# The edge stage of a graph layer: TensorE derives tile numbers in registers, ScalarE's copies take one loaded number a step

## The chip, the cores and the metric

The kernel runs on one core of a Trainium2 chip. The metric is the device time of one execution in microseconds (us). TensorE, VectorE, ScalarE and GpSimd are called PE, DVE, ACT and POOL, as in the profile; SP is the queue that only issues DMAs.
## The reference, cut to what matters

A layer over 6250 nodes with 512 features and 100000 edges sorted by their destination. It adds a graph attention term (the part at hand) and a linear attention term, and then a mixture of experts.

```
e      = leaky_relu(el[src] + er[dst])            # 8 heads
a      = exp(e - segment_max(e, dst)[dst])
denom  = segment_sum(a, dst);  msg = feat_v[src] * a / denom[dst]
x      = x + segment_sum(msg, dst) + linear_attention(layernorm(x))
x      = x + experts(layernorm(x))
```

## The kernel before, in words

Nodes are padded to 49 tiles of 128 rows (NT). Edges are cut into steps of 128 edges, so that no step crosses from one node tile into the next: 832 steps (ST), taken in 52 chunks of 16 (NCH, U). Tile numbers rise with the steps; a step that is the last of its tile is a "turn", and there are 48 turns inside the stage.

The program has a set-up, a projection of all 49 tiles (`proj`), a mix stage (`mix`), the **edge stage**, a join stage with routing, the experts and the output. The change is in the edge stage and in the tables that the set-up makes for it. Work in the edge stage is ordered by hand: every engine runs its own `chunk` function, a loop over two chunks a pass with the first and last two peeled (`chunks`, L114), and the engines meet at semaphores.

- POOL (`values`, L611 on, the DMA at L618) gathers 128 rows of `v_table` a step, 16 gathers a chunk into one half of `vg`. The gather for a step of chunk c waits for the same step of chunk c-2 on PE.
- DVE (`step`, L1186 on): every four steps it makes four one-hot matrices `hot` (L1189), and for each step it multiplies the gathered rows by their weights (L1182) and signals `step_pv`. Between the steps it runs the chain of small operations that makes the next chunk's weights: `scored` (after step 2), `run_max` (4), `linked` (6), `joined_max` (9), `shifted` (12), `factored` (14), `turned_hot` (15). `rescaled` (after step 1) takes the accumulator that PE closed with `acc_shut`, and scales it.
- PE (`step`, L1560 on): two f32 matmuls of 128x260 in four passes (L1566) add the step to the accumulator in one of two rooms of PSUM (tile number even or odd). It then branches on "turn" (L1569): a turn closes the room (`empty`, L1551) and opens the other. Between the steps PE does its part of the chain: `turned_e` (after step 1), `gathered_ends` (3), `spread_ends` (5), `turned_max` (8), `factors` (10). At a chunk's end it closes the accumulator for `rescaled`, and runs `expanded` for chunk c+2: 16 small matmuls, whose operand is addressed by the tile number of each step. At the next chunk's start it brings the scaled accumulator back in (L1581).
- ACT (`snapshots`, L748 on): for each step it copies an accumulator from PSUM to `fin` (L757). At a turn that is the finished tile; at any other step it copies a dummy bank, so that the program is the same for each. Before it the copy waits for four semaphores (L754 to L757). Between the copies ACT issues the loads of chunk c+2's locals and computes `factor` (after step 4, L741) and `weights` (after step 10, L745), which DVE needs for the next chunk's first step.
- SP (`tile_store`, L487) stores each finished tile from one of four slots of `fin`.

Numbers that depend on the data (where a step's accumulator lies, whether it is a turn, its tile) stand in tables in SBUF, one entry or more a step, and each engine loads them into registers with `looked_up` (L422, the load instruction has line L424):

```
marks[:] = looked_up(ENGINE.PE, pe_tab, t * 2, 2 * V + 1, 2 * D)        # PE: 9 numbers, 4 times a chunk
return looked_up(ENGINE.PE, d_tab, c * U, U, NT - 1)                     # PE: 16 numbers, once a chunk
places = looked_up(ENGINE.Activation, act_tab, t * 2, 2 * n, DUMMY * D)  # ACT: 2n numbers for n steps
counts = looked_up(ENGINE.Activation, act_tab, t * 2 + 2 * ST, 2 * n, 32768)
```

PE and DVE also load the chunks' base from `chunk_tab` (three numbers every two chunks), and PE loads one number at a turn. DVE makes the tables in the set-up (L943 to L984), 1x832 operations one behind the other.

## Time and profile before

| | us |
|---|---|
| median of 3 runs (lowest to highest) | 3522.52 (3513.96 to 3525.18) |
| the profiled execution, its own time | 3480.26 |
| its span, first to last instruction | 3478.4 |
| busy PE / DVE / POOL / ACT | 2417.5 / 1829.6 / 1338.1 / 909.8 |
| mean granted share of PE's clock | 0.809 |

The span is the time between the first and the last instruction of the profiled execution. Busy is the time in which an engine ran instructions; work of the sequencers is not counted in it. "Idle before" is the time in which an engine had nothing to run ahead of an instruction, with what ended it; "issue" there means that nothing which the profile shows was waited for, so that the engine's own sequencer was late. A granted clock of 1.00 is PE at full clock.

### The profile page before, as it was taken

Reading aid. Unit: us, or ns where it says so; the run is one execution under the profiler, and the core shown is the slowest. Engines: PE = TensorE matmul, PEld = TensorE weight load, DVE = VectorE, ACT = ScalarE, POOL = GpSimd, SP = SyncE. Lnnn points to the kernel's source line nnn. Section 1 sums busy time; section 2 is a strip of 40 time slices with the busy share of each in tenths; the row PEclk is TensorE's granted clock in tenths of the full one; section 3 lists DMA queues with packets and bytes.
Section 4 is the critical chain, followed back from the end, with each engine's and each line's share of the span. In section 5 each row is a group of like instructions: output and inputs, shape, how many; then the busy total and the mean of one; then the engine's idle time right before and its main releaser. Section 6 shows DMA issues by size and latency. Waiting matters only on the chain. (4 is left out here: it accounts for less than half of the span.)

```text
span 3478.4 us, 50828 instructions
## 1 busy us (share of the span) xinstructions
PE 2417.5 (69%) x11245; PEld 1803.3 (52%) x11246; DVE 1829.6 (53%) x3903; ACT 909.8 (26%) x1917; POOL 1338.1 (38%) x1406
## 2 busy tenths in 40 slices
PE   3899998666777877777877777777233329999500
PEld 3677776223555555555555555555233328888400
DVE  5544443786666655566556655565353334444433
ACT  0111111011333333333333333333443313333100
POOL 0000000302565555565556555652144342222244
PEclk8899998898888878888788878889555559999755
DMA  3122222644555555655656556653655634444576
GB/s 115 49 68 68 68 68 77 228 167 134 165 162 159 157 164 163 169 160 154 169 164 171 166 154 173 170 163 89 221 134 136 131 76 134 145 145 145 168 257 232
DMA packets 238264, 507.89 MB, mean 146 GB/s; under 512 B 50320, under 2 KB 76432, under 8 KB 238208
## 3 DMA queue, kind: packets, MB, share of 16 engines
q0 software_dynamic: 85936, 274.85, 28.6%
q1 hardware_dynamic: 134752, 196.94, 18.5%
q10 hardware_dynamic: 17520, 35.44, 3.0%
q8 instruction: 24, 0.39, 0.1%
q14 instruction: 32, 0.26, 0.0%
HBM read 394.73 MB, written 112.37 MB: 146 GB/s over the span
## 5 line engine op out<-in xcount | busy, mean ns | idle before, releaser
L618 POOL DMA_INDIRECT arena<-v_table,idx x832 | 917.2, 1102 | 847.1 <-PE ps L1566 670.1
L1566 PE MATMUL ps<-arena 128*128 128x260 f32 x3328 | 975.4, 441 | 315.9 <-issue 289.6
L1566 PEld LDWEIGHTS ps<-arena 128*128 128x128 f32 x3328 | 678.5, 216 | 533.2 <-issue 427.7
L757 ACT ACTIVATE arena<-ps x832 | 501.9, 603 | 1096.2 <-PE ps L1566 668.4
L1182 DVE TENSOR_TENSOR arena<-arena 128x512 f32<-128x512 f32 x832 | 547.1, 683 | 0.0
L1384 PE MATMUL ps<-arena 128*128 (+4 forms) x1994 | 423.8, 336 | 94.3 <-DMA arena<-q_table 73.8
L1389 PE MATMUL ps<-ident,arena 128*128 128x128 f32 x1128 | 213.8, 308 | 328.1 <-DVE arena L1257 257.2
L1384 PEld LDWEIGHTS ps<-arena 128*128 128x128 f32 (+1 forms) x1994 | 275.7, 195 | 224.8 <-issue 115.3
L1389 PEld LDWEIGHTS ps<-ident,arena 128*128 128x128 f32 x1128 | 151.0, 159 | 349.3 <-DVE arena L1257 262.2
L658 POOL DMA_INDIRECT arena<-xn_table,e_idx x105 | 99.3, 945 | 281.5 <-PE ps L1389 265.0
L595 POOL TENSOR_SCALAR ag<-ag 128x1 f32<-128x1 f32 x49 | 10.7, 219 | 502.3 <-DVE ag L999 502.2
L1189 DVE TENSOR_TENSOR arena<-col_no,arena 128x512 f32<-128x512 f32 x208 | 142.2, 684 | 106.2 <-ACT arena L745 55.2
L1336 DVE TENSOR_TENSOR xt_lo<-ps,xt_hi 128x512 fp32r<-128x512 f32 x105 | 72.6, 692 | 213.3 <-ACT xt_hi L824 213.3
L1182 DVE TENSOR_TENSOR arena<-ps,r_all 128x512 f32<-128x512 f32 x51 | 35.3, 692 | 219.2 <-PE ps L1551 219.2
L669 POOL DMA_INDIRECT arena<-y_table,slot_of x98 | 100.3, 1024 | 127.4 <-DVE arena L1375 74.8
L801 ACT ACTIVATE arena<-arena,r_den 128x64 f32<-128x64 f32 x392 | 98.6, 334 | 162.4 <-DVE r_den L1242 162.2
L1384 PE MATMUL ps<-w_hi,xt_hi 128*128 x420 | 129.1, 307 | 2.6 <-DVE xt_lo L1336 2.6
L1581 PE MATMUL ps<-arena,ident 128*128 128x260 f32 x204 | 103.3, 661 | 37.0 <-issue 32.3
L1239 DVE TENSOR_SCALAR r_den<-arena 128x8 f32<-128x8 f32 x49 | 8.4, 171 | 228.0 <-DMA arena<-agg 227.8
L1384 PE MATMUL ps<-w_hi,xt_lo 128*128 x420 | 119.5, 284 | 0.0
L1384 PE MATMUL ps<-w_lo,xt_hi 128*128 x420 | 118.2, 281 | 0.0
L635 POOL DMA_INDIRECT token_of<-token_no,slot_of x98 | 102.0, 1041 | 25.6 <-issue 25.6
(282 smaller groups left out, 3470.0 us busy)
## 6 DMA issues: line engine op xcount, KB each, us to landing
y_table<-arena SPq DMA_DIRECT2D x105, 256.0 KB, 2.5
arena<-local_table ACTq DMA_DIRECT2D x52, 512.0 KB, 4.2
arena<-in_x SPq DMA_DIRECT2D x98, 256.0 KB, 2.7
arena<-v_table,idx POOLq DMA_INDIRECT x832
v_table<-arena SPq DMA_DIRECT2D x49, 260.0 KB, 2.9
agg<-arena SPq DMA_DIRECT2D x49, 260.0 KB
arena<-agg SPq DMA_DIRECT2D x49, 260.0 KB, 4.6
x_mix<-arena SPq DMA_DIRECT2D x49, 256.0 KB, 2.7
```

The source lines that it names most:

```text
L618: pool.indirect_dma_start(vg[:, j % 2 * U + i, :], None, v_table, bass.IndirectOffsetOnAxis(ap=idx[:, j, i:i + 1], axis=0))\
L635: pool.indirect_dma_start(token_of, bass.IndirectOffsetOnAxis(ap=slot_of[:, t, k:k + 1], axis=0), token_no[:, t:t + 1], None).then_inc(s(" ...
L658: pool.indirect_dma_start(xg[:, j % 4, :], None, xn_table, bass.IndirectOffsetOnAxis(ap=e_idx[:, j:j + 1], axis=0)).then_inc(s(f"eg_in{j % ...
L669: pool.indirect_dma_start(cy[:, j * TOP + k, :], None, y_table, bass.IndirectOffsetOnAxis(ap=slot_of[:, t, k:k + 1], axis=0)).then_inc(s(f ...
L757: act.activation(halves(fin[:, bass.ds(dst_, DH)], HALF), halves(ps[:, bass.ds(src_, 2 * D)], D)[:, :, 0:HALF], ACT.Copy).then_inc(s("act_ ...
L801: last = act.activation(da[:, j, cols], da[:, j, cols], ACT.Copy, scale=r_den[:, j, h:h + 1])
L1182: return dve.tensor_tensor(out_[:, :, 0:D // 2].rearrange("p i (h f) -> p i h f", h=H // 2), in_[:, :, 0:D // 2].rearrange("p i (h f) -> p ...
L1189: dve.tensor_tensor(hot[:, i // V % 2], col_no[:].unsqueeze(1).broadcast_to([P, V, P]), dst_local[:, bass.ds(t, V)].unsqueeze(2).broadcast ...
L1384: last = pe.matmul(dst, a, b, start=(opened and i == 0), stop=(closed and i == n - 1))
L1389: last = pe.transpose(dst[:, c * P:(c + 1) * P], src[:, c * P:(c + 1) * P], ident[:])
L1566: last = pe.matmul(ps[:, bass.ds(acc + h * D, HALF)], hot[:, i // V % 2, i % V, :], vg[:, b * U + i, h * HALF:(h + 1) * HALF], start=False ...
L1581: pe.matmul(ps[:, bass.ds(base + h * D, HALF)], ident[:], acc_kept[:, h, :], start=True, stop=False)
```

## The change

Tables: `pe_tab`, `act_tab`, `d_tab` and `chunk_tab` go; `first_tab` (the tile of each chunk's first step), `turn_tab` (16 turn bits of each chunk) and `room_tab` (one number a step: the room at a turn, the dummy bank otherwise) come. `tile_tab` gets an entry ahead and an offset. PE works out each step's turn, tile and room from the chunk's first tile and its bits. ACT loads 16 numbers once a chunk; the number is the address of both source and target, so `fin` has two slots in place of four. The copy of step t waits for PE's step t+1, and no longer for `tile_sum` and `fin_st`; PE waits for `fin_st` at a turn instead. The chain operations stand at other steps. DVE's first `hot` of a chunk is ahead of the wait for the weights.

```diff
-def chunks(eng, body, bases=None):
+def chunks(eng, body, places, ahead):
     for c in range(2):
-        body(c, c, 0, *(bases(c, 2) if bases else ()))
+        body(c, c, 0, places(c, ahead + 1))
     with eng.Fori(1, NCH // 2 - 1) as i:
-        own = bases(i * 2, 3) if bases else ()
+        own = places(i * 2, ahead + 2)
         for j in range(2):
-            body(i * 2 + j, j, i, *own[j:j + 2])
+            body(i * 2 + j, j, i, own[j:j + ahead + 1])
...
+def turn_of(eng, bits, i):
+    return eng.snap((bits >> i) & 1, min_val=0, max_val=1)
+def room_of(eng, d):
+    return eng.snap((d & 1) * (2 * D), min_val=0, max_val=2 * D)
+def next_tile(eng, d, turn):
+    return eng.snap((d + turn).with_bounds(min_val=0, max_val=NT - 1))
...
+        def chunk_places(engine, c, n):
+            return list(zip(looked_up(engine, first_tab, c, n, NT - 1), looked_up(engine, turn_tab, c, n, 2 ** U - 1)))
...
-                sp.dma_start(rows(agg, d), fin[:, j * DH:(j + 1) * DH]).then_inc(s("fin_st"), 16)
+                sp.dma_start(rows(agg, d), fin[:, j * 2 * D:j * 2 * D + DH]).then_inc(s("fin_st"), 16)
...
-            def snapshots(t, n):
-                places = looked_up(ENGINE.Activation, act_tab, t * 2, 2 * n, DUMMY * D)
-                counts = looked_up(ENGINE.Activation, act_tab, t * 2 + 2 * ST, 2 * n, 32768)
-                for i in range(n):
-                    (src_, dst_), (closed, stored) = places[2 * i:2 * i + 2], counts[2 * i:2 * i + 2]
-                    act.wait_ge(s("step_mm"), t + (i + 1))
-                    if later(t, 1) or i:
-                        act.wait_ge(s("act_step"), t + i)
-                    act.wait_ge(s("tile_sum"), closed)
-                    act.wait_ge(s("fin_st"), stored)
-                    act.activation(halves(fin[:, bass.ds(dst_, DH)], HALF), halves(ps[:, bass.ds(src_, 2 * D)], D)[:, :, 0:HALF],
-                                   ACT.Copy).then_inc(s("act_step"), 1)
+            def snapshot(t, room):
+                if later(t, 1):
+                    act.wait_ge(*past("act_step", t))
+                act.wait_ge(s("step_mm"), t + 2)
+                act.activation(halves(fin[:, bass.ds(room, DH)], HALF), halves(ps[:, bass.ds(room, 2 * D)], D)[:, :, 0:HALF],
+                               ACT.Copy).then_inc(s("act_step"), 1)
...
+                rooms = looked_up(ENGINE.Activation, room_tab, c * U, U, DUMMY * D)
+                for i in range(U):
+                    snapshot(c * U + i, rooms[i])
+                    if not more:
+                        continue
+                    if i == 8:
+                        factor(c + 1)
+                    elif i == 11:
+                        weights(c + 1, 1 - b)
...
                 for i in range(U):
-                    step(c * U + i, i, b)
+                    if i % V == 0:
+                        found(c * U + i, i)
+                    if i == 0:
+                        dve.wait_ge(s("p_exp"), c + 1)
+                    step(i, b)
                     if i == 1 and later(c, 1):
-                        rescaled(c, base)
+                        rescaled(c, room_of(dve, own[0][0]))
...
-                    if i == 2:
+                    if i == 5:
                         scored(c + 1, n, q)
-                    elif i == 4:
+                    elif i == 7:
                         run_max(c + 1, n)
-                    elif i == 6:
+                    elif i == 9:
                         linked(c + 1)
-                    elif i == 9:
+                    elif i == 11:
                         joined_max(c + 1, n)
-                    elif i == 12:
+                    elif i == 13:
                         shifted(c + 1, n)
...
-                for i, d in enumerate(tiles):
+                for i in range(U):
                     last = product(prep[:, i * 3 * H:(i + 1) * 3 * H],
-                                   [(hot_t[:, i * P:(i + 1) * P], er_flat[:, bass.ds(d * 3 * H, 3 * H)])])
+                                   [(hot_t[:, i * P:(i + 1) * P], er_flat[:, bass.ds(d * (3 * H), 3 * H)])])
+                    if i < U - 1:
+                        d = next_tile(pe, d, turn_of(pe, bits, i))
...
-            def step(t, i, b):
-                if i % V == 0:
-                    marks[:] = looked_up(ENGINE.PE, pe_tab, t * 2, 2 * V + 1, 2 * D)
-                acc, turn, other = marks[i % V * 2:i % V * 2 + 3]
+            def step(t, i, b, d, turn):
+                acc = room_of(pe, d)
                 pe.wait_ge(s("step_pv"), t + 1)
...
+                other = ((acc + 2 * D) & (4 * D - 1)).with_bounds(min_val=0, max_val=2 * D)
                 with pe.If(turn):
-                    empty(acc, False, True).then_inc(s("tile_sum"), 1)
-                    freed, = looked_up(ENGINE.PE, pe_tab, t + (2 * ST + 2), 1, ST)
+                    empty(acc, False, True)
+                    pe.wait_ge(s("fin_st"), d * 16 + past("fin_st", -16)[1])
+                    freed, = looked_up(ENGINE.PE, tile_tab, d, 1, past("act_step", ST)[1])
                     pe.wait_ge(s("act_step"), freed)
                     empty(other, True, False)
...
-                    if i == U - 1 and ahead:
-                        tiles = tiles_of(c + 2)
-                    step(c * U + i, i, b)
+                    turn = turn_of(pe, bits, i)
+                    step(c * U + i, i, b, d, turn)
+                    d = next_tile(pe, d, turn)
                     if not more:
                         continue
-                    if i == 1:
+                    if i == 5:
                         turned_e(c + 1)
-                    elif i == 3:
+                    elif i == 7:
                         gathered_ends(c + 1)
-                    elif i == 5:
+                    elif i == 9:
                         spread_ends(c + 1)
-                    elif i == 8:
+                    elif i == 11:
+                        factors(c + 1)
+                    elif i == 12:
                         turned_max(c + 1)
-                    elif i == 10:
-                        factors(c + 1)
```

In the set-up, 23 operations over all 832 steps (L947 to L981) become 9, with a reduction to 52 numbers, 16 one-element memsets and a few small copies beside them.

## Rows read from the trace of the kernel before

**Rows 1.** The page: the span, and PE's granted clock in 40 slices, in tenths

```profile
span 3478.4 us, 50828 instructions
PEclk8899998898888878888788878889555559999755
```

**Rows 2.** Waits in the edge stage, 900 to 2370 us: total, times, longest

```profile
ACT arena L757 <- PE ps L1566: 598.4, 330, 6.9
POOL arena L618 <- PE ps L1566: 462.2, 288, 8.0
PE ps L1566 <- issue: 274.9, 186, 3.9
DVE arena L1182 <- PE ps L1551: 207.9, 47, 6.1
DVE arena L1130 <- DMA arena<-v_table,idx: 144.9, 47, 5.4
DVE arena L1189 <- ACT arena L745: 46.8, 24, 2.4
```

**Rows 3.** Line L424, one chunk, 1133 to 1163.5 us

```profile
L424 ACTq TENSOR_LOAD <-arena x11: 468/1717/1751, 1134.1 to 1163.4; - x11
L424 PEldq TENSOR_LOAD <-arena x7: 288/2157/3792, 1133.1 to 1157.6; - x7
```

**Rows 4.** Timeline of PE: start us, us, what, idle before in brackets

```profile
1120.33 1.92 PE L1566 MATMUL ps<-arena 128*128 128x260 f32 x8
1129.38 1.14 PE L1566 MATMUL ps<-arena 128*128 128x260 f32 x4 [2.93 <-issue]
```

**Rows 5.** Lines L1564 (in a PE step) and L1384 (in expanded), short windows

```profile
L1564 PEldq ALU_OP  x3: 36/36/36, 1155.5 to 1156.8; - x3
L1384 PEldq FUSED_REGOPS  x16: 64/64/74, 1130.3 to 1132.5; - x16
```

**Rows 6.** Line L1566: matmuls of 1138 to 1142 and of 1150 to 1153 us

```profile
L1566 PE MATMUL ps<-arena x8: 640/641/802, 1137.4 to 1141.9; 128*128 128x260 f32 x8
...
L1566 PE MATMUL ps<-arena x11: 382/383/482, 1149.7 to 1152.8; 128*128 128x260 f32 x11
```

**Rows 7.** Stretches of one chunk: busy of PE, PEld, DVE, ACT, POOL, PEclk, DMA

```profile
1124.00:1134.00 10.00, 5.87 (x34) 3.94 (x32) 3.84 (x8) 4.03 (x8) 6.94 (x8) 0.89 0.73 195
1134.00:1146.00 12.00, 10.92 (x27) 6.85 (x27) 4.87 (x12) 2.08 (x4) 2.86 (x3) 0.52 0.41 130
1146.00:1154.00 8.00, 7.42 (x33) 5.63 (x33) 7.37 (x20) 3.10 (x7) 5.99 (x5) 1.00 0.55 141
```

**Rows 8.** Groups of instructions in the edge stage, 900 to 2370 us

```profile
L1566 PE MATMUL ps<-arena 128*128 128x260 f32 x3020 | 893.0, 444 | 294.2 <-issue 274.9 <-DVE arena L1182 19.2
L618 POOL DMA_INDIRECT arena<-v_table,idx x753 | 834.7, 1108 | 621.0 <-PE ps L1566 462.2 <-issue 158.8
L757 ACT ACTIVATE arena<-ps x753 | 454.2, 603 | 1002.6 <-PE ps L1566 598.4 <-issue 214.4 <-ACT arena L757 82.8
L1182 DVE TENSOR_TENSOR arena<-arena 128x512 f32<-128x512 f32 x755 | 497.1, 683 | 0.0
L1159 DVE TENSOR_TENSOR_SCAN arena<-arena,f_l 128x128 f32<-128x128 f32 x47 | 22.8, 484 | 5.1
```

**Rows 9.** Line L745, one instruction a chunk, 52 in all

```profile
L745 ACT ACTIVATE arena<-arena x52: 301/301/310, 826.3 to 2407.1; 128x128 f32<-128x128 f32 x52
```

**Rows 10.** Timeline of DVE in the set-up: first and last operation on the tables

```profile
73.89 0.58 DVE L947 TENSOR_SCALAR arena<-arena 1x832 f32<-1x832 f32 x1
92.51 0.19 DVE L983 CAST arena<-ps 1x48 uint16<-1x48 f32 x1
```

**Rows 11.** Timeline at the end of the edge stage

```profile
2431.16 0.39 PE L1551 MATMUL ps<-zeros 1*128 1x260 bf16 x2
2438.36 0.60 ACT L757 ACTIVATE arena<-ps  x1 [0.66 <-ACT arena L757]
2441.02 5.67 SPq L500 DMA_DIRECT2D arena<-in_w  x4
```

More of the change, by code:

```diff
@@ L779, in _ @@
             weights(0, 0)
-            chunks(act, chunk)
+            chunks(act, chunk, lambda c, n: (None,) * n, 0)
             act.wait_ge(s("step_mm"), ST)
@@ L981, in _ @@
-            step_of(dve.tensor_copy(pe2[:, :, 1], turn))
+            step_of(dve.tensor_scalar(odd, odd, float(2 * D), -float(DUMMY * D), ALU.mult, ALU.add))
+            step_of(dve.tensor_tensor(odd, odd, turn, ALU.mult))
+            step_of(dve.tensor_scalar(room_tab[0:1, :], odd, float(DUMMY * D), None, ALU.add))
+            step_of(dve.memset(turn[:, ST - 1:ST], 0.0))
+            power_row, bits = odd[:, 0:U], odd[:, U:U + NCH]
+            for i in range(U):
+                last = dve.memset(power_row[:, i:i + 1], float(2 ** i))
@@ new lines, in _ @@
+            step_of(last)
+            in_chunks = [row_.rearrange("o (c i) -> o c i", i=U) for row_ in (turn, aux)]
+            step_of(dve.tensor_tensor(in_chunks[1], in_chunks[0], power_row.unsqueeze(1).broadcast_to([1, NCH, U]), ALU.mult))
+            step_of(dve.tensor_reduce(bits, in_chunks[1], AX.X, ALU.add))
+            dve.tensor_copy(turn_tab[0:1, 0:NCH], bits)
+            dve.memset(turn_tab[0:1, NCH:NCH + 2], 0)
+            dve.tensor_copy(first_tab[0:1, 0:NCH], d_r[:, 0:ST:U])
@@ L1226, in _ @@
             turned_hot(1, 1, 0)
-            chunks(dve, chunk, lambda c, n: looked_up(ENGINE.DVE, chunk_tab, c, n, 2 * D))
+            chunks(dve, chunk, lambda c, n: chunk_places(ENGINE.DVE, c, n), 0)
             def weights_lo(c):
@@ L1604, in _ @@
             pe.wait_ge(s("er_split"), 5)
[L1605 removed]
+            begun = chunk_places(ENGINE.PE, 0, 2)
+            expanded(0, *begun[0])
             turned_e(0)
@@ L1609, in _ @@
             turned_max(0)
-            expanded(1, tiles_of(1))
-            empty(0, True, False).then_inc(s("tile_sum"), 1)
-            chunks(pe, chunk, lambda c, n: looked_up(ENGINE.PE, chunk_tab, c, n, 2 * D))
-            empty((NT - 1) % 2 * 2 * D, False, True).then_inc(s("tile_sum"), 1)
+            expanded(1, *begun[1])
+            empty(0, True, False)
+            chunks(pe, chunk, lambda c, n: chunk_places(ENGINE.PE, c, n), 2)
+            pe.wait_ge(*past("fin_st", 16 * (NT - 2)))
+            empty((NT - 1) % 2 * 2 * D, False, True).then_inc(s("step_mm"), 1)
             def logits(t):
```

125 lines of the change are left out of this document (45 added, 80 removed).

## The prediction

> **What bounds the kernel now.** First the page: span 3478.4 us, with PE's granted clock at 0.8 to 0.9 of full through the edge stage [rows 1]. The execution's own time, 3480.3 us, is 42 us under the median of the runs, 3522.5; I make the sum against 3480.3 and move it by the difference. The line of `weights` comes once a chunk and gives the stage its measure: 1580.8 us for 51 intervals, **31.0 us a chunk** [rows 9].
>
> Then the waits, to see who is late [rows 2]. ACT and POOL wait for PE. DVE waits for PE too: 207.9 us, 4.4 a chunk, until PE has closed the accumulator. It also waits 3.1 a chunk for the gather, and 1.0 for ACT's exponential. PE waits for "issue", 274.9 us or 5.8 a chunk. Nothing else in the profile is late there: PE's own sequencer is. What it does shows on the load line, in one chunk [rows 3]. Four loads of nine numbers take 2.16 us each, one of 16 takes 3.79, one of a single number 0.29. That is about 0.23 us a number beyond the first, so the three-number load is near 0.75. Together 8.63 + 3.79 + 0.29 + 0.75 = 13.5 us of a 30.5 us chunk go to loading numbers. Some of it hides behind queued matmuls, but where matmuls are short or few, PE runs dry: 2.93 us before step 15, during the load of 16 [rows 4].
>
> ACT is second. It makes twelve loads a chunk: six of eight numbers at 1.72, four of two at 0.47 [rows 3], two of four at 0.88 between them; 14.0 us. With 16 copies at 0.60 [rows 8] that is 23.7 us before any wait, and so it is often behind.
>
> Last, the clock [rows 7]. Around the chunk's end PE has little work; after it, 12 us run at 0.52, near 1.2 GHz, and then 8 us at 1.00. A matmul takes 641 ns there and 383 ns else [rows 6]. The mean of 444 [rows 8] puts 24% of them, 15 of 64 a chunk, in the slow stretch. Back to back at full clock they come every (1.92 - 0.38)/7 = 0.22 us [rows 4], so 15 slow ones cost 3.3 us a chunk.
>
> **The change part by part.**
>
> *PE's loads.* Gone: 13.5 us a chunk, but for the one number at a turn. New: eight numbers every two chunks, as two loads of four, each 0.29 + 3 x 0.23 = 0.98, so 1.0 us a chunk. Net -12.2 us of sequencer.
>
> *PE's register work.* A step gains two operations for the turn bit, two for the room and one for the next tile; each of the 16 matmuls of `expanded` gains three. The trace has no bit operation, so I bound it. Below: register work that rides in one instruction with other register work is cheap, since the address instructions of `expanded` take only 64 to 74 ns where a single operation takes 36 [rows 5]; at some 12 ns an operation that is 0.06 us a step, 0.04 a small matmul. Above: each one alone. A single one takes 36 ns and a gap to the next instruction; the step's own four instructions recur every 0.65 us, a branch of 0.2 among them, so about 0.10 each, 0.5 a step and 0.3 a matmul; with two more for the other room, if they are made at each step, 0.7. I take 0.16 and 0.08, nearer the lower end, because rows 5 show compound register instructions wherever this kernel computes an address. Sum 16 x 0.24 = 3.8 us a chunk; bounds 1.6 and 16.
>
> PE's sequencer then: 30.5 less the waits, which I put at 3.8 in this chunk (what is left when steps at 0.65, loads and the rest are laid end to end), gives 26.7; minus 12.2, plus 3.8: **18.3 us**. It is no longer the limit.
>
> *What is late next.* PE's array: 64 matmuls at 0.22 are 14.1 us. Bringing the accumulator back is 0.9. `expanded` is 2.3 [rows 5] + 1.3. The five small products, the closings and the turn are about 4, an estimate from their 0.2 to 0.4 us a piece. That is **22.6 us** at full clock. On top come hand-overs. The chain operations used to stand three or four steps apart between PE and DVE (`turned_e` after step 1, `run_max` after 4; 8 and 12 for the maximum). They now stand two apart and finally one (12 and 13). So PE waits where DVE is inside `joined_max`: two scans of 0.48 and small ones, near 2 us, then one-hots and a product at 0.68 each [rows 8], while PE has one small product; 2.5 us. Likewise 1.2 us around `run_max`. Sum 3.7. Of the slow clock's 3.3 us I keep half, 1.7, because the thin stretch ahead of it shortens by the load of 16 and of three but does not go. New chunk: 22.6 + 3.7 + 1.7 = **28.0 us**, against 31.0.
>
> *ACT.* Loads 14.0 to one of 16 numbers: 0.47 + 14 x 0.21 = 3.4. Also 11 fewer address instructions and two fewer waits a step. It costs nothing as long as ACT stays behind PE: 3.4 + 9.7 + waits is far below 28. The load sits after the chunk's two DMA issues, so ACT starts each chunk some 5 us late; `factor` after copy 8 hides that. If the cover fails, `joined_max` waits for `factor`, which needs PE's step 9: 1 us at most, inside the 2.5 above. Copying a step later adds one step before a room is free; the shortest tiles are about 8 steps, so nobody waits. PE's new wait for `fin_st` asks for a tile stored two turns ago; queued behind it are the opening of the room and the next step, but the wait is met. Both 0.
>
> *DVE.* One-hots ahead of the wait for the exponential take up its 1.0 us. `scored` after step 5 instead of 2 gives the gather three more steps, about 2.6 us, against 3.1 us of wait. Both gains fall to DVE, which is not the bound; they are inside the 28.0 and I add nothing.
>
> *POOL and SP.* No instruction more. POOL is released by PE's steps and follows them. Its floor is 16 x (1.108 + 0.34 between two, 158.8/465) = 23.2 us a chunk [rows 2, 8], under 28.0. SP's stores are as many and as large.
>
> *Set-up.* The tables take 73.89 to 92.70, 18.8 us of DVE alone, with the first projection behind them [rows 10]. New: nine at 0.6 to 1.05 us, a reduction, 16 memsets and copies, 10.2 by those prices. **-8.6 us**; if the memsets cost 0.2 each, -6.
>
> *End of the stage.* PE's last instruction ends at 2431.6, ACT's last copy at 2439.0, and SP's weight loads start at 2441.0 [rows 11]. With ACT one copy behind PE, that shrinks from 7.4 to about 1: **-6.4 us**. Behind it is the last tile's store, as before.
>
> Sum: 51 x 3.0 = 153, + 8.6 + 6.4 = **168 us**; 3480.3 - 168 = 3312, and by the same 168 from the median, **3354 us**.
>
> **The rivals.**
>
> *A. PE stays at full clock and the chunk falls to POOL's pace.* The thin stretch is shorter, and if that is enough for PE never to fall to 1.2 GHz, the slow clock's rest goes too, and with loosely coupled hand-overs the chunk meets POOL's 23.2 to 25 us. For: 5.8 us a chunk of issue waits go. Against: `expanded` with its few columns stays, and 2 us of waiting are added in the middle. Time: 31.0 - 24.5 = 6.5 x 51 = 332 + 15: 3175 us.
> The Trainium skill ("TensorE: Matmul & The Clock Gate", Part 1) says the array's slow clock is the default and that only activity lifts it. By that rule a denser PE gains beyond the time saved; the rows 7 agree that thin work precedes the slow stretch, and whether it is thin enough here no row of the kernel before can say.
>
> *B. The hand-overs eat it.* The closer chain costs 6 us and the slow clock stays whole: 22.6 + 5.5 + 3.3 is 31.4, no gain in the stage. For: DVE already waits for PE at 4.4 us a chunk. Time: the ends alone, 3507 us, and up to 3525.
>
> *C. Slower: register work takes the loads' place.* Mechanism: bit operations don't join others, so that a step's sequence is 0.65 + 0.7 us, above the array's 0.88. PE's sequencer is then 26.7 - 12.2 + 16 = 30.5 us a chunk with nothing prefetchable, and about 2 us of the hand-overs lie bare: 32.5, +1.5 x 51 - 15 = +61: 3584 us. It decides from about 0.6 us of added register time a step. For: no row shows a bit operation. Against: rows 5.
>
> That the change doesn't do what it says is no case of weight: the loads go, by the code.
>
> **How the numbers follow.** Forecast 0.51 (27 to 30 us a chunk: 3305 to 3455), A 0.21, B 0.14, C 0.14. A measurement here tells about 0.3%, 10.5 us, from no change. Faster: forecast, A, and about half of B (3507 is 0.4% down) = 0.79; same 0.07; slower 0.14. The range of eight in ten reaches from **3200**, which leaves out the lower part of A, to **3520**, the middle of B; the forecast alone is 3305 to 3455.
>
> **What would show it.** Right: loads of PE and ACT down to under 1.5 and 3.5 us a chunk; `weights` every 28 us; PE's "issue" waits mostly gone; new waits of PE for DVE's `joined_max` and of DVE for PE's transposes; tables at 10 us; ACT's last copy 1 to 2 us after PE. If step-to-step on PE's sequencer is over 1.1 us, C is at work. If the chunk is under 26 us and the clock near 1.00, A. If the chunk is 31 with loads gone, B, and the wait that holds it is on the list of waits by name. The prediction is wrong in kind if ACT, slowed by its one load, holds a room that PE needs.

## The result, and the profile after

The changed kernel is **slower**: 3643.24 us in the median of four runs (3637.65 to 3653.28) beside 3518.80 (3513.96 to 3525.18) for the kernel before, a ratio of 1.036 with a 95% interval of 1.032 to 1.039. (The 3522.52 from which the prediction starts is the median of three of the same four runs.) The forecast was 3354 in a range of 3200 to 3520.

One warning on the sets of runs. Each set ran on one chip, with the kernel before beside it. In this set and in the fifth below the kernel before took 3512 to 3519 us, in the four between (on three chips) 3478 to 3485. The changed kernel stood at 1.036 here and, measured twice more, at 1.014 and 1.013 on chips of the other kind. The profiled execution of before took 3480.3 us, so its trace is comparable with the traces of the four sets between. Below, the sign and the mechanism are read from those, and the first trace of the changed kernel is given beside them.

The page of the changed kernel's first trace, its span, clock, and the groups that answer to [rows 8]; the last line is the scan that begins DVE's part of the chain:

```profile
span 3635.5 us, 53428 instructions
...
PEclk8999997997888887887878888878755558999855
...
L637 POOL DMA_INDIRECT arena<-v_table,idx x832 | 860.6, 1034 | 1070.5 <-PE ps L1563 837.3
L1563 PE MATMUL ps<-arena 128*128 128x260 f32 x3328 | 990.5, 451 | 180.2 <-DVE arena L1180 98.3
...
L770 ACT ACTIVATE arena<-ps x832 | 502.7, 604 | 1250.9 <-PE ps L1563 945.5
...
L1180 DVE TENSOR_TENSOR arena<-arena 128x512 f32<-128x512 f32 x832 | 539.0, 684 | 0.0
...
L1133 DVE TENSOR_TENSOR_SCAN arena<-arena,ps 128x128 f32<-128x128 f32 x52 | 21.9, 421 | 406.1 <-issue 259.1
```

The work is the same. DVE's and ACT's operations take as long as before; the matmul's mean is 451 ns, after 441 on the page of before (444 in the window of [rows 8]), and the gather's 1034 after 1102 there. POOL and ACT mainly wait longer. The line of `weights`, in the first trace of the changed kernel and then in its third measurement, on a chip where before takes 3478:

```profile
L764 ACT ACTIVATE arena<-arena x52: 301/302/310, 827.3 to 2577.3; 128x128 f32<-128x128 f32 x52
```

```profile
L764 ACT ACTIVATE arena<-arena x52: 301/302/310, 818.6 to 2470.2; 128x128 f32<-128x128 f32 x52
```

That is (2577.3 - 827.3)/51 = **34.3 us a chunk** and (2470.2 - 818.6)/51 = **32.4**, against 31.0 [rows 9] and the 28.0 of the forecast. The loss is there. In the third measurement, on a chip like that of before's trace, the span grew by 45.9 us (3524.3 for 3478.4): the 51 intervals give 70.8, the first `weights` comes 7.7 earlier, and what follows the last one is 17.2 shorter. The first trace's span grew by 157 us with 51 x 3.3 = 168 in the intervals, but it is from the chip on which before itself takes 38 us more, so that sum holds the chip's part too.

What took the place of the old waits? The waits of the edge stage, 900 to 2300 us, in the third measurement (us in total, times, longest):

```profile
ACT arena L770 <- PE ps L1563: 900.1, 343, 11.8
POOL arena L637 <- PE ps L1563: 523.6, 271, 10.8
DVE arena L1133 <- PE ps L1533: 340.6, 43, 11.8
...
PE ps L1563 <- DVE arena L1180: 152.4, 95, 2.7
...
DVE carry L1150 <- ACT factor_h L760: 70.1, 43, 3.4
DVE arena L1162 <- PE ps L1545: 69.4, 43, 3.3
...
PE ps L1582 <- issue: 58.9, 29, 2.8
PE ps L1386 <- issue: 47.0, 284, 0.3
...
DVE arena L1180 <- PE ps L1552: 30.8, 28, 3.0
...
PE ps L1563 <- issue: 0.5, 3, 0.2
```

PE's "issue" waits in the steps are gone, 0.5 us where [rows 2] have 274.9, and DVE hardly waits for the closed accumulator (30.8 for 207.9). At the end of a chunk PE still waits for its own sequencer: 1.4 us a chunk before the scaled accumulator is brought back (58.9 us; 30.0 before, 0.6 a chunk) and 1.1 in `expanded` (47.0). In place of the old waits stands a chain of hand-overs: DVE waits 7.9 us a chunk (340.6/43.2) for PE's turned scores, 1.6 for ACT's factor, 1.6 for PE's turned maximum, and PE 3.5 for DVE's products. In the kernel before, DVE's wait for the factor was next to nothing, 0.07 us a chunk. The same row of its waits, 900 to 2370 us:

```profile
DVE carry L1152 <- ACT factor_h L741: 3.5, 5, 1.1
```

The sequencer of PE in the changed kernel: the branch at the end of a step, in steps that follow one another, and the register work of `expanded` (a chunk's 16 small matmuls):

```profile
L1567 PEldq COMPARE_BRANCH  x8: 207/207/207, 1688.4 to 1695.5; - x8
...
L1386 PEldq ALU_OP  x29: 3/36/341, 1613.8 to 1618.9; - x29
L1386 PE MATMUL ps<-arena x16: 173/184/200, 1614.0 to 1619.1; 128*128 x16
```

Steps recur every (1695.5 - 1688.4)/7 = 1.01 us, small matmuls every (1619.1 - 1614.0)/15 = 0.34, where [rows 5] give 2.2/15 = 0.15.

The loads, over 900 to 2400 us, PE's and ACT's:

```profile
L439 PEldq TENSOR_LOAD <-arena x80: 3/981/997, 965.8 to 2389.1; - x80
...
L439 ACTq TENSOR_LOAD <-arena x44: 3374/3400/4355, 905.7 to 2387.6; - x44
```

Set-up and end of the stage, to [rows 10, 11]: the first and the last operation on the tables, then PE's last instruction and SP's weight loads.

```profile
73.65 0.58 DVE L957 TENSOR_SCALAR arena<-arena 1x832 f32<-1x832 f32 x1
...
82.57 0.20 DVE L981 TENSOR_SCALAR arena<-ps 1x48 uint16<-1x48 f32 x1
...
2598.34 0.39 PE L1552 MATMUL ps<-zeros 1*128 1x260 bf16 x2
...
2602.09 2.08 SPq L519 DMA_DIRECT2D arena<-in_w  x3
```

The tables take 9.1 us for 18.8, the stage's end 3.8 for 9.9. Both are close to the prediction (9.7 us gained for 8.6, 6.1 for 6.4), and the 16 memsets are one row of 0.21. But on the first chip the first `weights` starts at 827.3 for 826.3: nothing of the 9.7 us reached the edge stage there, while in the third measurement it starts at 818.6.

### The profile page after: what moved, and what is told of

Same layout as the page of the kernel before. It is cut to its first block, busy times and chain, and to the rows that moved or that the text cites. A ratio compares the mean times of both kernels' runs of the same rounds, so it can differ in the third digit from the quotient of the medians.

```text
span 3635.5 us, 53428 instructions
## 1 busy us (share of the span) xinstructions
PE 2503.5 (69%) x11245; PEld 1857.2 (51%) x11246; DVE 1828.1 (50%) x3907; ACT 911.4 (25%) x1917; POOL 1288.9 (35%) x1406
## 3 DMA queue, kind: packets, MB, share of 16 engines
q1 hardware_dynamic: 134752, 196.94, 17.7%
## 4 chain that ended last, share of the span: by engine, by line
PE 23%; DMA 9%; issue 8%; DVE 8%; POOL 1%; SPq 1%; another core or an unknown queue 1%; ACT 1%; ACTq 1%; DVEq 0%; POOLq 0%
PE ps L1386 11%; PE ps L1563 9%; DMA arena<-agg 5%; DMA arena<-y_table,slot_of 3%; PE ps L1391 2%; DVE arena L1180 1%; DVE bn L1252 1%; PE ps L1582 1%; POOL arena L688 1%; DVE arena L1250 1%; PE ps L1552 1%; DVE arena L1259 1%; DVE arena L1374 1%; DVE arena L1377 1%
## 5 line engine op out<-in xcount | busy, mean ns | idle before, releaser
L637 POOL DMA_INDIRECT arena<-v_table,idx x832 | 860.6, 1034 | 1070.5 <-PE ps L1563 837.3
L1563 PE MATMUL ps<-arena 128*128 128x260 f32 x3328 | 990.5, 451 | 180.2 <-DVE arena L1180 98.3
L1563 PEld LDWEIGHTS ps<-arena 128*128 128x128 f32 x3328 | 711.3, 225 | 380.5 <-issue 258.0
L1386 PE MATMUL ps<-arena 128*128 (+4 forms) x1994 | 495.6, 336 | 228.8 <-issue 96.7
L1180 DVE TENSOR_TENSOR arena<-arena 128x512 f32<-128x512 f32 x832 | 539.0, 684 | 0.0
L1386 PEld LDWEIGHTS ps<-arena 128*128 128x128 f32 (+1 forms) x1994 | 296.4, 192 | 404.1 <-issue 313.6
L1133 DVE TENSOR_TENSOR_SCAN arena<-arena,ps 128x128 f32<-128x128 f32 x52 | 21.9, 421 | 406.1 <-issue 259.1
```

The source lines that it names most:

```text
L637: pool.indirect_dma_start(vg[:, j % 2 * U + i, :], None, v_table, bass.IndirectOffsetOnAxis(ap=idx[:, j, i:i + 1], axis=0))\
L1180: return dve.tensor_tensor(out_[:, :, 0:D // 2].rearrange("p i (h f) -> p i h f", h=H // 2), in_[:, :, 0:D // 2].rearrange("p i (h f) -> p ...
L1386: last = pe.matmul(dst, a, b, start=(opened and i == 0), stop=(closed and i == n - 1))
L1563: last = pe.matmul(ps[:, bass.ds(acc + h * D, HALF)], hot[:, i // V % 2, i % V, :], vg[:, b * U + i, h * HALF:(h + 1) * HALF], start=False ...
```

## The experiments

Two theories to begin with. **The order**: the chain's places were moved, so that PE and DVE stand two steps apart and less, and the hand-overs lie bare. **The register work**: bit operations that stand alone take the place of the loads. Each run's chunk is the span of its `weights` line over 51, read from one trace. The edits are shown in short form.

### First set: which part of the change costs (before: 3484.65 us)

**e1_moved**, the kernel before with the five places of PE and of DVE and the two of ACT as the change has them, and PE's loads as before. ACT's numbers are the same 64 a chunk, but in ten loads for twelve, since its copies are grouped around other places:

```diff
 PE:   i == 1, 3, 5, 8 (maximum), 10 (factors)  ->  5, 7, 9, 12 (maximum), 11 (factors)
 DVE:  i == 2, 4, 6, 9, 12                      ->  5, 7, 9, 11, 13
 ACT:  factor after copy 4, weights after 10    ->  factor after copy 8, weights after 11
```

> The kernel before, with only the places of the chain operations moved as the change moves them (PE 5, 7, 9, 11, 12; DVE 5, 7, 9, 11, 13; ACT's factor after copy 8, its weights after copy 11); tables and loads as before. The changed kernel's chunk is 34.3 us against 31.0, +3.3, though its sequencer's loads went. Theory O (order): the closer hand-overs cost the time, so this kernel is slower than before as well, by 3 us a chunk or more: over 3670 us against 3519. Theory R (register work): the order is worth nothing or a gain, and the register instructions cost the time: 3519 within 1%, or below. If both have a share, it lies between, and the share is read off.

Measured: 3568.44 us, 1.024 (1.022 to 1.026), chunk 32.75. The order costs 1.75 us a chunk without any of the register work.

**e2_order_back**, the changed kernel at the old places:

```diff
-    PE 5, 7, 9, 11 (factors), 12 (maximum); DVE 5, 7, 9, 11, 13; ACT factor after copy 8, weights after 11
+    PE 1, 3, 5, 8 (maximum), 10 (factors); DVE 2, 4, 6, 9, 12; ACT factor after copy 4, weights after 10
```

> The changed kernel, with the chain operations back at their old places (PE 1, 3, 5, 8, 10; DVE 2, 4, 6, 9, 12; ACT 4 and 10). Theory O: the hand-overs loosen, and what is left is the gain of the loads: 28 to 30 us a chunk, 3360 to 3460 us. Theory R: a chunk stays near 34 us, 3640 us within 1%, because PE's step has a pitch of 1.02 us in its sequencer where it had 0.61, and a small matmul of the expansion 0.34 where it had 0.14, wherever the chain stands.

Measured: 3411.30 us, 0.979 (0.977 to 0.980), chunk 30.04. Its wait of PE for the joined maximum and of DVE for the factor, 900 to 2300 us:

```profile
PE ps L1545 <- DVE arena L1157: 111.9, 47, 4.2
...
DVE carry L1150 <- ACT factor_h L760: 71.1, 39, 3.1
```

The rest of the change is a gain once the places are the old ones. But DVE's wait for the factor is already here, 1.5 us a chunk, so it isn't only the order that makes it.

**e3_arith**, the changed kernel with the bit operations written as arithmetic:

```diff
-    (bits >> i) & 1          (d & 1) * (2 * D)   (acc + 2 * D) & (4 * D - 1)
+    bits // 2 ** i % 2       (d % 2) * (2 * D)   acc * -1 + 2 * D
```

> The changed kernel, with the shift and the bit operations written as divisions, remainders and products, which can share one register instruction. Theory R: the steps' pitch falls from 1.02 toward 0.8 us, the small matmuls' from 0.34 toward 0.25, some 5 us a chunk off the sequencer, and most of it shows: 3400 to 3500 us. Theory O: the chunk gains less than 1.5 us, since PE's sequencer waits in the hand-overs: above 3560 us.

Measured: 3537.06 us, 1.016 (1.014 to 1.017), chunk 32.29. The changed kernel itself had 32.40 and 1.014 in the next set. Cheaper register work brings next to nothing in the changed order.

**e4_pe_loads**, the changed kernel with PE's numbers loaded from tables again; `step` takes three numbers of nine, `expanded` 16 tile numbers. The eight numbers every two chunks of the changed kernel stay beside them (before loads three there), and a turn loads two numbers for one:

```diff
-                acc = room_of(pe, d)
+                if i % V == 0:
+                    marks[:] = looked_up(ENGINE.PE, pe_tab, t * 2, 2 * V + 1, 2 * D)
+                acc, turn, other = marks[i % V * 2:i % V * 2 + 3]
```

> The changed kernel, with PE's numbers loaded from tables again (nine numbers four times a chunk, sixteen once), and ACT's single load, two slots and the new order kept. Theory R: PE's register work is gone, ACT is relieved: at or below the kernel before, 3400 to 3520 us. Theory O: the new order alone makes it slow: above 3600 us, since the loads come back on top.

Measured: 3582.20 us, 1.029 (1.027 to 1.030), chunk 33.26: 0.86 over the changed kernel, 0.51 over e1_moved. Against e1_moved it has ACT's new part, and no gain of it shows. What the 0.51 belongs to isn't separated: PE's further loads come to some 0.9 us of its sequencer a chunk, an estimate from the 0.98 us of a load of four, the 0.75 of one of three and the 0.29 of one number.

### Second set: the lead, and what each part brings in the old order (before: 3482.11 us)

**e5_after**, the changed kernel itself, no edit.

> The changed kernel itself, beside the others on one chip, so that all stand against the same kernel before. 34.3 us a chunk, ratio 1.036 as before; no theory expects otherwise.

Measured: 3533.70 us, 1.014 (1.013 to 1.016), chunk 32.40. The loss is real on this chip too, but under half of what the first one showed.

**e6_loose**, PE's places earlier, DVE's left as changed:

```diff
-    PE 5, 7, 9, 11 (factors), 12 (maximum); factor after copy 8
+    PE 4, 6, 8, 9 (factors), 10 (maximum);  factor after copy 6
```

> The changed kernel, with DVE's chain as late as the change puts it (5, 7, 9, 11, 13), but PE's share earlier, at 4, 6, 8, 9 and 10 in place of 5, 7, 9, 11 and 12, and ACT's factor after copy 6 in place of 8. So DVE may again be three steps ahead of PE where it had two, and in the end one. Theory L (lead): the new order costs time because DVE may not run ahead of PE far enough: this gives most of the 4.3 us a chunk back, 30 to 31.5 us a chunk, ratio 0.98 to 1.00. Theory D (depth): it costs because the chain begins so late that it ends past the chunk, whatever the lead: 33 to 34.3 us a chunk, ratio above 1.02.

Measured: 3409.85 us, 0.979 (0.978 to 0.981), chunk 29.92: all that e2_order_back gives.

**e7_loads_back** is e4_pe_loads at the old places (diffs of e4_pe_loads and e2_order_back).

> PE's numbers loaded from tables, the old order, ACT's single load: so the kernel before with the new ACT part and set-up. If ACT's loads had a part in the 31.0 us, this is below before: 29 to 30.5 us a chunk, ratio 0.96 to 0.98, and then PE's registers bring nothing by themselves beside the 30.0 us of the changed kernel in old order. If PE's sequencer alone was the bound, it stays at 30.5 to 31.5, ratio 0.99 to 1.01, and the 1.0 us gained is the registers'.

Measured: 3504.35 us, 1.006 (1.005 to 1.008), chunk 31.63. It is the kernel before with the new set-up, DVE's one-hots and ACT's part, and with more loads on PE: 322 in 900 to 2300 us, 7.3 a chunk, where before has 288, 6.4 a chunk. Its chunk is 0.6 us longer than the 31.0 of before. So eleven loads less a chunk on ACT show no gain, though PE's extra loads may hide one. From here to e2_order_back (30.04) it is 1.6 us a chunk for PE's registers; from the kernel before, with its fewer loads, to e2_order_back it is 1.0.

**e8_arith_back** is e3_arith at the old places.

> The old order with division and remainder in place of shift and bit operations. In the new order that rewriting was worth 2.0 us a chunk. If PE's sequencer is still in the path in the old order, it gives 1 to 2 us again: 28 to 29 us a chunk, ratio 0.95 to 0.965. If the path now runs through the array, DVE and the hand-overs, under 0.5 us: ratio 0.97 to 0.98.

Measured: 3380.77 us, 0.971 (0.969 to 0.973), chunk 29.32. In the old order the cheaper register work is worth 0.7 us a chunk; in the changed one 0.1. The branch of its steps, one after the other:

```profile
L1567 PEldq COMPARE_BRANCH  x7: 203/207/207, 1601.7 to 1606.9; - x7
L1567 PEldq FUSED_REGOPS  x6: 107/107/107, 1601.5 to 1606.0; - x6
```

A step takes (1606.9 - 1601.7)/6 = 0.87 us of the sequencer for 1.01.

### Third set: which hand-over (before: 3478.92 us)

**e9_turn4** moves one place of PE, **e10_max10** two, **e11_arith_loose** joins e3_arith and e6_loose, and **e12_inif_back** is e8_arith_back with the other room computed inside the branch:

```diff
 e9:   -    i == 5: turned_e                  +    i == 4: turned_e
 e10:  -    i == 11: factors, 12: turned_max  +    i == 9: factors, 10: turned_max
 e12:  -    other = (acc * -1 + 2 * D) ...    (ahead of the branch)
       +        other = (acc * -1 + 2 * D) ...    (in it)
```

> The changed kernel with one place altered: PE turns the scores over after step 4, not 5; the other four places of PE stay. The profile of the changed kernel has DVE standing 338.3 us (7.2 a chunk) at the running maximum until that turn, and PE standing 153.6 us for DVE's products. Theory of the lead (the first hand-over carries it: what DVE loses there PE pays back later in the chunk): the turn comes one step earlier, about 1 us a chunk of DVE's stand goes, and the chunk falls from 32.4 to about 31.4, ratio to before about 1.00. Rival (the last hand-over carries it, the maximum turned after step 12 right behind the factors): the first place is worth nothing, the chunk stays at 32.4, ratio 1.014. Theory of the register work (PE's sequencer paces): no change either.

Measured: 3542.65 us, 1.019 (1.017 to 1.020), chunk 32.59. No gain. Its waits, 900 to 2300 us, say where it went:

```profile
DVE arena L1133 <- PE ps L1533: 286.1, 42, 10.6
...
DVE carry L1150 <- ACT factor_h L760: 118.2, 43, 4.1
```

DVE's largest wait fell from 7.9 to 6.7 us a chunk, and its wait for ACT's factor rose from 1.6 to 2.8. The wait of 7.9 us, which I had taken for the cost, can thus be cut by 1.2 without a gain, as long as the factor comes late. ACT comes next.

> The changed kernel with the end of the chain alone brought forward on PE: factors after step 9, behind the spread ends, and the turned maximum after step 10, not 11 and 12. Theory of the first hand-over: DVE makes the maximum at its step 11 only, after its long stand, so PE now waits for it at step 10 with nothing gained for DVE; chunk 32.4 or some tenths more, ratio 1.01 to 1.02. Rival (last hand-over): DVE's stand for the turned maximum (64.9 us, 1.4 a chunk) and PE's stand at the steps behind it (153.6 us, 3.3 a chunk) go, chunk about 30, ratio about 0.98.

Measured: 3483.03 us, 1.002 (1.001 to 1.003), chunk 31.46. The rival's direction, at two fifths of its size.

> Two edits of earlier runs together: the five places of PE brought forward (0.979 alone) and the bit operations written as division, remainder and product (1.0156 against 1.0143 in the changed order, so nothing there; 0.971 against 0.979 in the old order). If the register work counts only where the hand-overs leave PE the last to arrive, this order gives what the old one gave: about 0.971, chunk 29.2. If the places brought forward have made DVE the last to arrive, the register work is hidden and it stays at 0.979, chunk 29.9.

Measured: 3393.85 us, 0.976 (0.974 to 0.977), chunk 29.64: between the two.

> The fastest version so far (old order, arithmetic in place of bit operations, 0.971, chunk 29.3) with the two operations for the other room moved into the branch that needs them, so that only a turn makes them. It takes about 2 x 0.1 us from PE's sequencer at 14 or so of 16 steps, 2.9 us a chunk. Theory of the register work: PE's sequencer still sets part of the chunk, 0.5 to 1.5 us a chunk go, ratio 0.95 to 0.965. Rival (the array and the hand-overs set it): within 0.3% of 0.971.

Measured: 3374.10 us, 0.970 (0.969 to 0.972), chunk 29.32. Void as a test of register work: the order of instructions on PE is the same as in e8_arith_back, as far as the traces show: both have 50007 instructions, and ahead of each branch the same one of 107 ns. It stands as a second measurement of the fastest version.

### Fourth set: the place of ACT's factor (before: 3478.31 us)

```diff
 e13_factor6, on the changed kernel:
-                    if i == 8:
+                    if i == 6:
                         factor(c + 1)
```

**e14_factor6_max10** adds e10's edit to it; **e15_loose_factor8** is e6_loose with the factor left after copy 8; **e16_after** is the changed kernel.

> The changed kernel with ACT's factor after copy 6 instead of 8, nothing else. Copy 8 needs PE's step 9, and DVE's joined maximum behind its step 11 needs that factor: where PE's turn was moved to step 4, DVE's stand for the factor grew from 1.70 to 2.75 us a chunk and ate what was won. Theory of the closed ring (PE step 9, ACT's copy and factor, DVE's joined maximum and next product, PE step 12): the 1.7 us stand of DVE goes and with it 1 to 2 us of PE's 3.55 a chunk for products; chunk 31.2 to 31.8 against 32.4, ratio 0.99 to 1.00 where the changed kernel has 1.014. Rival (only the last hand-over, the turned maximum after step 12, carries it): no gain, within 0.3% of the changed kernel.

> Factor after copy 6 and the end of the chain early on PE (factors after 9, turned maximum after 10) together; the first three places as changed (5, 7, 9). The maximum alone gave 32.4 to 31.46. If the ring and the last hand-over are two separate costs they add: about 30.5, ratio 0.985 to 0.99. If the first three places also count, something is left against the 29.92 (0.979) of all places moved. If the end of the chain was the whole cost, 29.9.

> All five places of PE early (4, 6, 8, 9, 10) with ACT's factor left after copy 8. Theory of the ring: DVE stands for the factor by 2 us or more a chunk instead of 1.0, the chunk is 30.5 to 31.5 against 29.92 with factor after copy 6; ratio 0.99 to 1.005. Rival (ACT's place does not matter): 0.979.

> The changed kernel itself again, as the base for this set: it stood at 1.0356 in its first measurement and at 1.0143 in the second. Chunk 32.4, ratio 1.014 to 1.018 if the second is typical, 1.03 or over if it varies from set to set.

Measured: **e13_factor6** 3436.91 us, 0.988 (0.986 to 0.990), chunk 30.70; **e14_factor6_max10** 3418.68, 0.982 (0.981 to 0.984), chunk 30.24; **e15_loose_factor8** 3477.93, 1.000 (0.999 to 1.001), chunk 31.37; **e16_after** 3525.51, 1.013 (1.011 to 1.015), chunk 32.38.

One digit takes the changed kernel from 1.3% slower than before to 1.2% faster. Left late while all of PE's places are early (e15 against e6, from another chip), it costs 1.45 us a chunk. DVE's wait for the factor, 900 to 2300 us, in e13_factor6 and in e15_loose_factor8, to be held against 70.1 us above:

```profile
DVE carry L1150 <- ACT factor_h L760: 12.6, 19, 1.4
```

```profile
DVE carry L1150 <- ACT factor_h L760: 123.7, 45, 4.1
```

Why is the factor late after copy 8? ACT in one chunk of e16_after, in order of time:

```profile
1606.56 0.60 ACT L770 ACTIVATE arena<-ps  x1 [10.93 <-PE ps L1563]
1612.08 0.60 ACT L770 ACTIVATE arena<-ps  x1 [4.92 <-PE ps L1563]
1612.90 0.60 ACT L770 ACTIVATE arena<-ps  x1 [0.21 <-PE ps L1563]
1613.72 0.60 ACT L770 ACTIVATE arena<-ps  x1 [0.21 <-ACT arena L770]
...
1618.62 0.60 ACT L770 ACTIVATE arena<-ps  x1 [0.21 <-ACT arena L770]
1619.12 0.18 ACT L760 ACTIVATE factor_h<-factor_h 8x1 f32<-8x1 f32 x1
```

The load of ACT's 16 numbers in the same chunk:

```profile
L439 ACTq TENSOR_LOAD <-arena x1: 3408/3408/3408, 1608.3 to 1608.3; - x1
```

And PE and DVE around it:

```profile
1614.12 2.18 PE L1563 MATMUL ps<-arena 128*128 128x260 f32 x8 [1.14 <-DVE arena L1180]
1616.22 0.40 PE L1386 MATMUL ps<-g_lk,sel_t 8*128 8x32 f32 x2
1616.67 2.14 PE L1563 MATMUL ps<-arena 128*128 128x260 f32 x8
1619.87 0.38 PE L1386 MATMUL ps<-diag,hot_first 8*128 8x8 f32 x2 [1.06 <-DVE hot_first L1152]
1622.92 1.39 PE L1563 MATMUL ps<-arena 128*128 128x260 f32 x4 [2.66 <-DVE arena L1180]
```

```profile
1619.34 0.14 DVE L1150 COPY carry<-g_lk 8x1 f32<-8x1 f32 x1 [2.45 <-ACT factor_h L760]
```

The copy at 1606.56 is the last of the chunk before. The change made each copy wait for one step more, so this one waits 10.9 us for PE to get through `expanded` and into the next chunk. Only then come the two DMA issues and the load, 3.4 us: the chunk's first copy is at 1612.08, when PE has done six steps. ACT then copies as fast as it can, every 0.82 us, and is through copy 8 and the factor at 1619.3. PE's step 9, for which copy 8 asks, ended at 1614.12 + 2.18 = 1616.3. So it is ACT's backlog, not PE, that sets the factor here. The hand-overs close a ring: PE's step, ACT's copy and factor, DVE's joined maximum and next product, PE's later step. DVE stands 2.45 us for it at its joined maximum, its products for PE's last steps are late by that, and PE stands 1.06 before the factors and 2.66 before step 12.

Is it the late place or ACT's new part that makes DVE wait? Its wait for the factor, 900 to 2300 us, in e1_moved (late place, old part), e7_loads_back (old place, new part) and e4_pe_loads (late place, new part):

```profile
DVE carry L1151 <- ACT factor_h L741: 51.9, 43, 2.0
```

```profile
DVE carry L1157 <- ACT factor_h L762: 60.4, 41, 2.4
```

```profile
DVE carry L1157 <- ACT factor_h L762: 84.5, 42, 4.1
```

That is 1.2, 1.4 and 2.0 us a chunk, for 0.07 before. Either one without the other already goes with the wait. No run moved the load or the added step of lag alone; that they make the backlog is read from the rows of e16, that the factor's place is worth 1.7 us a chunk is shown.

### Fifth set: the same ring in the old order (before: 3512.39 us, the slower kind of chip)

**e17_back_factor3** is e12_inif_back, **e18_back_factor6** is e2_order_back, each with one digit changed (factor after copy 3, and after copy 6, for 4).

> The fastest version (old places, arithmetic in place of bit operations, other room in the branch; 0.9705, chunk 29.32) with ACT's factor after copy 3 instead of 4. It still has DVE standing 1.38 us a chunk for the factor and PE 2.39 for the joined maximum behind it. Theory of the ring: the ring closes here too, PE step, ACT's copy and factor, DVE's joined maximum, PE's turned maximum after step 8; 0.5 to 1 us a chunk go, ratio 0.955 to 0.965. If factor at copy 3 then waits for DVE's own linked maxima (its step 6) the gain is smaller, down to nothing. Rival (in the old order the ring is open enough): within 0.3% of 0.9705.

> The changed kernel at the old places (0.979, chunk 30.0) with ACT's factor alone put back by two copies, from 4 to 6: the same two copies that were worth 1.7 us a chunk in the changed order. Theory of the ring: PE stands at its turned maximum after step 8 for DVE's maximum, which stands for the factor, which stands for PE's step 7; the ring closes over two steps and costs 1.5 to 3 us a chunk, chunk 31.5 to 33, ratio 1.00 to 1.025. Rival (the factor's place matters only among the changed places): 0.98 to 0.985.

Measured: **e17_back_factor3** 3445.79 us, 0.980 (0.977 to 0.984), chunk 30.54; **e18_back_factor6** 3638.31, 1.034 (1.032 to 1.037), chunk 34.42. Waits of e18_back_factor6, 900 to 2300 us:

```profile
DVE carry L1150 <- ACT factor_h L760: 136.2, 39, 4.4
PE ps L1386 <- issue: 121.4, 241, 2.2
...
PE ps L1545 <- DVE arena L1157: 98.6, 24, 5.5
```

With e18 the direction is as the ring has it, and so is the place: DVE's wait for the factor is 3.3 us a chunk (136.2/40.7) for 1.5. The size can't be split, since the versions they differ from ran on the other kind of chip, where the changed kernel itself stands 2% better against before. For the same reason e17 decides nothing: 0.980 here is not to be compared with 0.970 there.

## Why the prediction was wrong

**ACT: "`factor` after copy 8 hides that ... 1 us at most ... Both 0."** This is the step that failed. I had seen that ACT starts each chunk some 5 us late, and took it as harmless. Nine copies at 0.82 us follow before the factor, while PE takes a little over 1 us a step, so by copy 8 about 2.3 us of the lateness are left (1618.6 for 1616.3), and these DVE waits for. I also costed the copies' extra step of lag only by the rooms it holds, not by what is queued behind it on ACT: the load. In the kernel before, the chunk's first loads (two of 1.73 and 1.75 us, from 1134.1 on, in the chunk of [rows 3]) were through before PE had ended its first step at 1138.9. Measured: 1.7 us a chunk for the place alone (e13), where the sum had nothing of its own. That is 1.7 of the 4.4 us a chunk by which 32.4 exceeds the forecast's 28.0; the rest lies with the points below, and isn't split among them. And "costs nothing as long as ACT stays behind PE" is not borne out: the versions with the new ACT part are 0.5 to 0.6 us a chunk slower (e4 over e1, e7 over before), though PE's extra loads, DVE's one-hots and the set-up differ too, and how much is ACT's stays open.

**The hand-overs, 3.7 us.** The waits foreseen are there: PE for DVE around the joined maximum, DVE for PE's transposes. As a term of the sum they were too small. The changed places cost 2.36 us a chunk against the old ones (32.40 - 30.04), where the forecast had them inside a gain of 3. I set them beside the old load waits instead of laying the ring end to end, over PE, ACT and DVE. Taken one after the other, the factor's place is worth 1.68, then the end of the chain on PE 0.46 (e14), then PE's first three places 0.32 (e6, on another chip). The split depends on the order: with the end of the chain first it is 0.92 for that (e10) and 1.22 for the factor (e14).

**The end of a chunk on PE.** I said of PE's sequencer that it is no longer the limit, from a sum over the whole chunk. At the chunk's end it still is. The small matmuls of `expanded` take 15 x 0.34 + 0.18 = 5.3 us where the sum of 22.6 had 2.3 + 1.3. And the two loads of four, every second chunk, lie bare: in e16_after PE's last small matmul ends at 1599.8, the loads run from 1600.2 to 1602.3, and the next matmul is this one:

```profile
1602.58 2.10 PE L1582 MATMUL ps<-arena,ident 128*128 128x260 f32 x4 [2.75 <-issue]
```

The row of waits above gives 1.4 us a chunk for it. Both rows stay at the old places (63.3 and 47.1 us in e2_order_back), and the sum of 28.0 has no room for them. No run took them away alone, so what they cost the whole isn't shown.

**PE's loads and registers.** The loads went as foreseen, 1.0 us each and two every two chunks. The register work is 0.4 us a step for the 0.16 taken, and 0.19 a small matmul for 0.08: 16 x 0.59 = 9.4 us for 3.8, in the middle of the bounds of 1.6 and 16. Bit operations do stand alone, 36 ns each; rows of compound address instructions were the wrong neighbours for them. Yet the trade is still a gain in the old order, 1.0 us a chunk with the rest of the change (before to e2) and 1.6 from e7, and making the dearer work cheaper brought next to nothing in the changed one (e3). Rival C came nearest in time, 3584 for 3643: +61 us, where +124 was measured here and +47 and +52 in the later sets. That was luck: a step took 1.01 us, under its mark of 1.1, and e3 says that the steps' register work wasn't what held the chunk.

**Rival B** was the right one in kind, hand-overs that eat the gain, and at 31.4 us a chunk too mild. It had no ACT in it.

**The clock.** I kept half of 3.3 us. The mean matmul of 451 ns puts (451 - 383)/(641 - 383) = 26% of them in the slow stretch for 24%: nothing was given back. The groups of the steps' matmuls, 900 to 2300 us, in e16_after and e13_factor6:

```profile
L1563 PE MATMUL ps<-arena 128*128 128x260 f32 x2747 | 817.1, 452 | 154.9 <-DVE arena L1180 152.4 <-issue 0.5
```

```profile
L1563 PE MATMUL ps<-arena 128*128 128x260 f32 x2905 | 806.6, 426 | 130.1 <-DVE arena L1180 124.5 <-issue 2.7
```

With PE's stands shorter the mean falls by 26 ns, to 17% slow ones. Matmuls overlap, so the price is read from the busy time: 817.1 us over 43.2 chunks and 806.6 over 45.6 are 18.9 and 17.7 a chunk, 1.2 less. PE's wait for DVE's products fell by 0.8 a chunk. The two together, 2.0, come to a little more than the 1.7 gained, so they are no clean sum. A wait in the middle of the steps is thus paid for partly as matmuls at 1.2 GHz: in the chunk of e16_after shown above PE is busy for 2.3 of the 6 us from 1618 to 1624, and its granted clock, 1.00 at the start of them, is 0.50 from 1624 to 1626. How much each of the two carries was not separated. The Trainium skill ("TensorE: Matmul & The Clock Gate", Part 1) has the slow clock as the default that activity lifts, and this pair agrees in direction.

**DVE, POOL, SP, set-up, end.** DVE's exponential wait went, and the wait for the gather with it (3.0 us in all of e16), for no gain, as said. POOL and SP as said. Set-up 9.7 for 8.6 and end 6.1 for 6.4.

The ledger over the chips where before takes 3480 or so: 31.00 us before; + 0.63 for the new ACT part with DVE's one-hots and PE's extra loads (e7); - 1.59 for PE's registers in place of all those loads (e2); + 2.36 for the changed places (e5), of which 1.68 go by moving the factor's alone: 32.40.

The best version run is the changed kernel at the old places with arithmetic for bit operations, 0.971 and 0.970 of before in two sets. The forecast's 0.952 was not reached by any: its chunk of 28.0 is 1.3 us below the best one run.

## What to carry to other kernels

When a step of a chain over several engines is moved, write the ring out once round, with each engine's backlog at that point, and ask of every hand-over not only who waits but how far behind its own queue the giver runs. A load or an issue is free only at a place where its engine would idle; a wait added ahead of it can take that idle time away. The longest wait on the list need not be the cost: here the one of 7.9 us could be cut by 1.2 for nothing, and moving the hand-over behind the one of 1.6 gave 1.7. A sequencer that is idle on the average over a chunk can still be the limit at one place of it.

## What the runs showed that I had not expected

The size of the loss differs between the sets, each of which ran on one chip. The changed kernel lost 3.6% on one and 1.3 to 1.4% on two others, while before differs by only 1%. In the first trace most of DVE's 406.1 us ahead of the scan, and 65.5 us ahead of PE's steps in 900 to 2400 us, are put down to "issue"; on the other chips those of PE are 0.5 and 0.8 us in 900 to 2300. What differs stays open.

Single register operations are not cheap by being small: at 36 ns each they took some 0.1 us of PE's sequencer apiece (the trace shows five of them in a step for one before, and the step grew by 0.4 us). Written as division and remainder they show as compound instructions of 107 ns, and a step fell from 1.01 to 0.87 us.
